# A fused adaLN, Mamba-2 and FFN kernel on one core: a new order of the last prologue steps and of the first unit's state updates

## The reference

```
mod = silu(c) @ wmod                                    # six rows of 512: sa ca ga sb cb gb
ga, gb = sign * max(|.|, 0.25)
h   = layernorm(x) * (1 + ca) + sa
proj = h @ in_proj_w.T                                  # gate 8192 | hBC 8192 + 1024 + 1024 | dt 128
hBC = silu(causal_conv4(hBC) + conv_b)                  # -> hs (128 heads x 64), B, C (8 groups x 128)
dt  = clip(softplus(dt + dt_bias), 0, 100);  A = -exp(A_log)
Y   = chunked scan, chunks of 128 tokens:
      Y_diag = (C B^T * L) (dt hs);  states = B^T (decay * dt hs);  Y_off = exp(A_cum) C state
y   = (Y + D hs) * silu(gate), RMS-normalised in 8 groups of 1024 channels, * norm_w
x   = x + ga * (y @ out_proj_w.T)
x   = x + gb * ((layernorm(x)*(1+cb)+sb) @ sign(ffn_w).T + ffn_b)
```

## Time and profile before

| | |
|---|---|
| median of three runs | 1803.72 us |
| profiled execution, its own time | 1806.34 us |
| its span, first to last instruction | 1804.5 us |
| TensorE matmul busy | 1738.3 us, 96% of the span |
| TensorE weight load busy | 1361.5 us, 75% |
| VectorE / ScalarE / GpSimd busy | 1379.1 / 1078.1 / 977.6 us |
| granted TensorE clock, mean | 0.985 of full |

### The profile page before, as it was taken

The page is one execution under the profiler, slowest core; times in us unless marked ns, Lnnn a source line. Parts: engine busy times, 40 slices in busy tenths (PEclk is TensorE's granted clock), DMA queues, the critical chain, the costliest instruction groups (busy, mean ns, idle before and its releaser), DMA issues.

```text
span 1804.5 us, 31771 instructions
## 1 busy us (share of the span) xinstructions
PE 1738.3 (96%) x9818; PEld 1361.5 (75%) x9818; DVE 1379.1 (76%) x2266; ACT 1078.1 (60%) x1830; POOL 977.6 (54%) x732
## 2 busy tenths in 40 slices
PE   6789999999999999999999999999999999999988
PEld 4567778777777777777787777777777777877776
DVE  4767788777877788777887778777887778876776
ACT  6556665666556666565656665566665656465553
POOL 1436474555546565355646555455754556676651
PEclk9899999999999999999999999999999999999989
DMA  6312121121212122021211212121210212221111
GB/s 229 103 37 70 50 79 45 36 68 56 80 29 74 45 66 63 27 74 56 68 52 36 69 50 79 29 74 51 69 55 26 74 56 74 78 62 60 51 47 59
DMA packets 80936, 112.97 MB, mean 63 GB/s; under 512 B 28402, under 2 KB 32498, under 8 KB 79988
## 3 DMA queue, kind: packets, MB, share of 16 engines
q1 hardware_dynamic: 62898, 78.24, 14.7%
q10 hardware_dynamic: 17858, 32.52, 5.4%
HBM read 88.42 MB, written 22.29 MB: 61 GB/s over the span
## 4 chain that ended last, share of the span: by engine, by line
issue 46%; POOL 36%; PE 10%; ACT 3%; DVE 2%; DMA 1%; SPq 1%; POOLq 1%; ACTq 0%; DVEq 0%
POOL yt L1798 10%; POOL ssq L1793 7%; POOL prev L1775 6%; POOL wg_lo L1700 4%; POOL wo_lo L1700 3%; POOL yt L1801 3%; POOL wx_lo L1700 3%; PE bank L506 2%; PE bank L508 2%; PE bank L507 2%; PE bank L895 1%; PE bank L767 1%; PE bank L902 1%; DMA gate<-w_mod_dram 0%; DMA dtw_d<-xdt 0%
## 5 line engine op out<-in xcount | busy, mean ns | idle before, releaser
L1798 POOL TENSOR_TENSOR yt<-yt,ea 128x384 f32<-128x384 f32 (+1 forms) x128 | 189.7, 1482 | 378.9 <-DVE ea L1608 378.9
L1578 DVE TENSOR_TENSOR lm<-lm,cbm 128x512 f32<-128x512 f32 x256 | 189.4, 780 | 147.7 <-ACT lm L1179 146.9
L1375 DVE SCALAR_TENSOR_TENSOR xc<-bank,bpar,xc 128x511 f32<-128x511 f32 (+2 forms) x384 | 285.3, 743 | 6.8
L506 PE MATMUL bank<-h_hi,wg_hi 128*128 128x512 f32 x640 | 262.0, 409 | 20.3 <-ACT gate L1104 10.4
L508 PE MATMUL bank<-h_hi,wg_lo 128*128 128x512 f32 x640 | 251.1, 392 | 0.0
L507 PE MATMUL bank<-h_lo,wg_hi 128*128 128x512 f32 x640 | 250.4, 391 | 0.0
L1775 POOL TENSOR_TENSOR prev<-prev,dec 128x512 f32<-128x512 f32 x96 | 130.5, 1360 | 154.7 <-DVE prev L1521 92.2
L506 PE MATMUL bank<-h_hi,wx_hi 128*128 128x512 f32 x512 | 211.2, 413 | 2.2 <-DVE bt L1375 2.2
L506 PE MATMUL bank<-wo_hi,g_hi 128*128 128x512 f32 x496 | 206.5, 416 | 0.0
L508 PE MATMUL bank<-h_hi,wx_lo 128*128 128x512 f32 x512 | 201.0, 393 | 0.0
L507 PE MATMUL bank<-h_lo,wx_hi 128*128 128x512 f32 x512 | 200.1, 391 | 0.0
(11 more groups left out here) (222 smaller groups left out, 3943.4 us busy)
## 6 DMA issues: line engine op xcount, KB each, us to landing
raw_w<-w_in_dram SPq DMA_DIRECT2D x145, 256.0 KB, 2.7
raw_w<-w_out_dram SPq DMA_DIRECT2D x64, 256.0 KB, 2.6
part_d<-part ACTq DMA_DIRECT2D x64, 256.0 KB, 2.1
part<-part_d ACTq DMA_DIRECT2D x60, 256.0 KB, 2.7
rt<-rows_d SPq DMA_DIRECT2D x256, 6.0 KB
acc<-x_dram SPq DMA_DIRECT2D x8, 256.0 KB, 6.9
acc<-w_mod_dram SPq DMA_DIRECT2D x2, 1024.0 KB, 6.1
lh<-neg_d SPq DMA_DIRECT2D x128, 6.0 KB
```

The source lines that it names most:

```text
L506: nc.tensor.matmul(out_ap, whi(k), hhi(k), start=(k == 0), stop=False)
L1375: stt(dst[:, at], ps[:, 0:HALF - 3 + k], w(k), dst[:, at], ALU.mult, ALU.add)\
L1578: tt(lm[:, h % 4, :], lm[:, h % 4, :], cbm[:, toks(hf)], ALU.mult).then_inc(v_m, 1)
L1798: tt(yt[:, j % 2, cols], yt[:, j % 2, cols], ea[:, j % 2, cols], ALU.add).then_inc(p_t3, 1)
```

## The change

Nothing is added or removed; the same instructions stand in another order.

- SyncE: weight fill 8 is issued ahead of the store of `dtw_d` and of the wait for it, fills 9 and 10 behind the last store of the decay rows and ahead of the wait for all these stores and of the 13 loads of `unit_params`.
- TensorE: projections 6 and 7 (x tiles 2 and 3) stand ahead of modulation row 5. In unit 0 the fourth gate projection and `gate_rows` stand ahead of state 0.
- ScalarE: the copy of row 5 stands behind the taps of x tiles 2 and 3; the weight splits 9 and 10 and the silu calls around them change places.
- VectorE: in unit 0 the low part of `xw` stands ahead of the state addition of the round before.
- GpSimd: weight tiles 9 and 10 are lowered ahead of the product for `gate_rows`.

```diff
--- before.py
+++ after.py
@@ -404,6 +404,7 @@
             store_rows(0, 1)
             sp.wait_ge(a_row, 7)
             store_neg(1)
+            pro_fill(8)
             sp.wait_ge(v_dtt, 4)
             sp.dma_start(dtw_d.rearrange("b t f w n -> t b (f w n)"),
                          flat(xdt, 0, 4).rearrange("t (b n) -> t b n", b=NBLK)).then_inc(d_scrt, 16)
@@ -411,18 +412,17 @@
             store_rows(0, 2)
             sp.wait_ge(d_scrt, 16)
             unit_steps(0, 0)
-            pro_fill(8)
             sp.wait_ge(p_split, 4)
             store_neg(2)
             sp.wait_ge(a_row, 8)
             store_rows(1, 1)
             sp.wait_ge(p_split, 5)
             store_rows(1, 2)
+            for n in range(9, FILLS0):
+                pro_fill(n)
             sp.wait_ge(a_const, 5)
             sp.wait_ge(d_scr, 16 * 20)
             unit_params(0, 0)
-            for n in range(9, FILLS0):
-                pro_fill(n)
 
             def x_tile(t):
                 if t >= 2:
@@ -613,10 +613,10 @@
             mod_row(4, 6)
             pro_item(5)
             to_tokens(1)
+            pro_item(6)
+            pro_item(7)
             te.wait_ge(a_mrow, 5)
             mod_row(5, 6)
-            pro_item(6)
-            pro_item(7)
             te.wait_ge(v_dtt, 4)
             for v in range(2, 6):
                 mod_columns(v, 4)
@@ -777,7 +777,8 @@
                 for z in range(NZ):
                     transposes(z)
                     if z == 2:
-                        gate_proj(g, c, 3)
+                        if not first:
+                            gate_proj(g, c, 3)
                         states(1)
                         continue
                     if z == 3:
@@ -796,9 +797,10 @@
                             if c in (0, 3):
                                 sum_squares(g - 1 if c == 0 else g, 1 if c == 0 else 0)
                     if z == 1:
+                        if first:
+                            gate_proj(g, c, 3)
+                            gate_rows()
                         states(0)
-                        if first:
-                            gate_rows()
 
                 items = early(proj_items(c, last))
                 order = [it for step in items for it in step]
@@ -1064,10 +1066,10 @@
             keep_row(4)
             pro_split(7)
             pro_tap(5)
-            keep_row(5)
             pro_split(8)
             pro_tap(6)
             pro_tap(7)
+            keep_row(5)
             def part_at(g, c):
 
                 return (g - 1, 1, 1) if c == 0 else (g, (c - 1) // 2, (c - 1) % 2)
@@ -1107,11 +1109,11 @@
             silu_x(0, 0)
             silu_x(0, 1)
             silu_c(0)
+            pro_split(9)
+            silu_gate(0, 0, 0)
             silu_x(0, 2)
-            silu_gate(0, 0, 0)
-            pro_split(9)
+            pro_split(10)
             silu_x(0, 3)
-            pro_split(10)
 
             def unit(g, c, last, first):
                 u, nb, hf = UPG * g + c, 2 * g + c // 2, c % 2
@@ -1555,11 +1557,13 @@
                         tt(by_head(xw[:, z % 2, :]), src, heads(dtw[:, hf], 1, z), ALU.mult).then_inc(v_xw, 1)
                     if z == 3 and not first:
                         accumulate(u, g1, b1, h1, 2, end)
-                    if z >= 1:
+                    if z >= 1 and not first:
                         new_state(z - 1)
                     if not last and z < NZ - hf:
                         ve.wait_ge(a_xh, sb0 + z + 1)
                         tt(xw_lo[:, z % 2, :], xw[:, z % 2, :], xw_hi[:, z % 2, :].bitcast(F), ALU.subtract).then_inc(x_lo, 1)
+                    if z >= 1 and first:
+                        new_state(z - 1)
                     if not first:
                         if z == 0:
                             group_sums(u, g1, b1, h1)
@@ -1743,11 +1747,10 @@
             tt(neg_parts[2], row_parts[1], fx, ALU.subtract).then_inc(p_split, 1)
             po.wait_ge(a_row, 8)
             tt(exp_parts[2], fy, exp_parts[1], ALU.subtract).then_inc(p_split, 1)
-            pro_lower(7, 9)
+            pro_lower(7, FILLS0)
             po.wait_ge(v_gval, 1)
             tt(flat(ea, 0, 2).rearrange("p (i n) -> p i n", n=128), ident[:, :].unsqueeze(1).broadcast_to((128, 2 * NK, 128)),
                small[:, 16:16 + 2 * NK].unsqueeze(2).broadcast_to((128, 2 * NK, 128)), ALU.mult).then_inc(p_diag, 1)
-            pro_lower(9, FILLS0)
             po.wait_ge(t_mrow, 6)
             nc.gpsimd.memset(flat(acc, 0, NT), 0.0).then_inc(p_zero, 1)
```

## The result

| | before | changed |
|---|---|---|
| median (6 runs each) | 1805.51 us | 1796.22 us |
| range | 1803.08 to 1807.29 | 1794.12 to 1798.02 |
| profiled execution, own time / span | 1806.34 / 1804.5 us | 1795.91 / 1794.1 us |
| mean granted clock | 0.985 | 0.989 |

The ratio is 0.9947, interval 0.9937 to 0.9957: 9.3 us off, 7.8 to 11.4. Forecast were 6.0 us off; the direction and the range held, the size was too small by a third. The forecast time, 1797.7 us, lies nearer to the measured 1796.22 than that only because the median of the kernel before is 1.8 us higher over six runs than over the three that the forecast started from.

The account below looks back on a forecast made before the run. TensorE, almost unbroken from 150 us, was taken as the bound, so only earlier time counted. Terms 3.3 + 2.44 + 0.7 - 0.5 = 5.9, say 6.0 us, gave 1803.72 - 6.0 = 1797.7 us; range 1794.0 to 1802.5.

Parts of the forecast that it names:

- The bound: From 150 us TensorE works almost without a break, so a shift of that stretch's entry shifts the end equally.
- Part 1: Prologue: two x projections ahead of modulation row 5 use most of TensorE's 4.48 us pause; gain 3.3 us.
- Part 2: Prologue: earlier fills 9 and 10 remove TensorE's whole wait ahead of the third gate projection; gain 2.44 us.
- the fills aren't there: Rival: fills 9 and 10 land past 89 us, the third gate projection's wait stays; 1800.1 us, chance 0.07.
- Part 3: Unit 0: the reordered chain puts the last state T + 14.0 behind the transposes, against 14.86; 0.7 us taken.
- The price against it: Unit 0: gaps ahead of states 2 and 3 make the clock fall earlier; a loss of 0.5 us, from 0 to 4.
- slower, by the states: Rival: clock falls at about 98 us in unit 0, low until about 125; 1807.7 us with Part 1 cold, chance 0.08.
- it goes deeper: Rival: the clock stays up through the columns and the states; up to 9 us, 1794.7 us, chance 0.08.
- The sum: Start of unit 1's x projections: 3.3 + 2.44 + 0.7 - 0.5 = 5.9, say 6.0 us, and the same at the end.
- The exchange on VectorE: Unit 0, low part before state addition: by VectorE/GpSimd exclusion worth nearly its cost; without it, about 1 us loss.

Follow-up runs that it names:

- `spread_columns`: Changed kernel with column products dealt out between gate projection k-steps, fills 9 and 10 ahead of the last neg_d stores: 1793.75 us.
- `old_unit0`: Changed kernel with unit 0 as before (fourth gate projection between states 0 and 1, state additions ahead of low parts): 1798.97 us.
- `warm_gaps`: Changed kernel with 6 unused matmuls ahead of state 2 and 6 ahead of state 3 of unit 0: 1794.70 us.
- `before_warm_gaps`: Kernel before with 4 unused matmuls ahead of state 2 and 6 ahead of state 3 of unit 0: 1804.60 us.
- `no_fill8`: Changed kernel with weight fill 8 back in its old place behind the load of step sizes: 1800.37 us.
- `both`: Changed kernel with `spread_columns`' edit, unit 1's first x projection ahead of unit 0's state 3, and 6 unused matmuls ahead of state 2: 1790.92 us.
- `old_row_order`: Changed kernel with modulation row 5 ahead of x projections 2 and 3, and its copy ahead of tile 8's split, as before: 1799.86 us.

## Why the prediction was right or wrong

- **The bound.** Right: the shift at 124 us (8.95) is there at 1547 us (8.70), and TensorE is as busy in the steady stretch (198.08 of 200 us). 0.25 us were lost on the way.
- **Part 1, 3.3 us.** Right in size: 76.92 - 73.19 - 0.26 = 3.5 us, and 3.3 when undone. The size has some luck in it. It was worked out from a return of the clock 3.5 to 4.4 us behind the start of dense work, and the clock does not go by that (last section); where it came back at 70.7 or 70.9 instead of 68.3, in `spread_columns` and `old_unit0`, row 5 started at 73.39 and 73.48 instead of 72.19, and 1.2 us of the gain were not there. Wrong was the sentence that the early fill 8 costs and brings nothing, "even as late as before": I looked at TensorE's gate projection, which was in time, and not at what the split holds up on ScalarE now that the row's copy stands behind it. Without that fill 4.16 us of wait appear.
- **Part 2, 2.44 us.** The wait went as forecast and the fills landed as forecast (83 to 85; their splits began at 82.90 and 84.43). But its price was read off as the wait's length in the kernel before. That holds only while nothing ahead of it moves. With part 1 done, the late fills would have waited away part 1 as well; with late fills the third gate projection starts only 0.5 us earlier than before, and the ratio is 0.9999. Parts 1 and 2 are worth some 6 us together and part 1 close to nothing alone. The rival "the fills aren't there", at 1800.1 us, counted part 1 as won; that kernel took 1804.87.
- **Part 3, 0.7 us.** A mis-sized term: 1.5 us, with the cost of the new low stretch in it. State 0 came 5.3 us behind the transposes and not 5.6, and a round took 3.19 us and not 3.35; the low parts took 0.69 us each and GpSimd's three decays 1.06 (1.56, 1.44 and 1.06 before).
- **The price against it, -0.5 us.** The step that failed. I had the clock fall earlier, which it did, and priced the new low stretch; that price was near (0.8 us by `warm_gaps`, and part 3's 1.5 has it in it already). But I set nothing against it for the old low stretch that goes away. That one lay over x projections, of which 2.5 us ran cold; the new one lies over short products that wait for others anyway. From the first x projection to the second off-diagonal product it is 6.01 us instead of 7.17: +1.2 where the sum has -0.5, a miss of 1.7 us. `old_unit0` (7.29) shows it again, and `before_warm_gaps` (5.99) that it is the clock's. The prediction knew of this cost, put it at 3.3 us in its rival "slower, by the states", and left it out of its own sum. What that rival feared, a low clock from 98 to 125, did not come: no low stretch of the 14 kernels outlasted 10.2 us.
- **The rival "it goes deeper".** Its 9 us are close to the 9.3, but by luck: the clock did not stay up through the columns and the states (low from 75.2 to 82.0 and from 102.5 to 109.3).
- **The sum.** At the second off-diagonal product, with the 0.26 us taken off: row and columns 3.5 - 0.4 (the columns took 5.1 us and not 4.7; the clock fell in their midst in both kernels, so why is open), from there to the B/C products 0.3, from those to the third gate projection 2.7, the chain of states 1.5, the clock behind it 1.2: 8.7 (the parts rounded), of which 8.4 are left in the last group, against 6.0. The rest of the 9.3 of the runs lies within their interval. The prediction read the falls of the clock before as 79.5 and 113.4 us; its windows give 79.1 and 113.2, but no term of the sum rests on these.
- **The exchange on VectorE.** Its mechanism, exclusion, is seen again in both kernels with the old order in the last rounds; the claim that the old order in rounds 2 and 3 costs nearly what it saves is right for state 3 (0.4 us) and the x projections (0.0).

## What to carry to other kernels

A wait is worth its length only if nothing ahead of it gets faster. Of two waits in a row the second swallows what the first gave, if what ends it comes no earlier; so removals are to be priced together and undone one by one. When an instruction is moved behind a load's consumer on its engine, that load can join the path. And a low clock costs by what lies in it: here 1.2 us for 2.5 us over dense matmuls, 0.8 for 6.8 us over a chain of short products that wait anyway. A low stretch that goes away is to be priced like one that comes. A stretch of pauses is best kept away from the start of dense work, or filled with some of that work.

## What the runs showed of the hardware

The column products of one column each did not keep the clock up, though TensorE counts as busy in them: in the twelve kernels where they stood in a row it fell 2.0 to 3.2 us after the first of them, or 5.2 where a wait parted them (`no_fill8`); dealt out between matmuls of 512 columns, in `spread_columns` and `both`, they left it high.

The clock's return is the second point. I had taken the clock's return for a delay behind the start of dense work (3.5 and 4.4 us in the prediction). The windows of all 14 kernels (the two compared and the twelve of the experiments) between 55 and 135 us say otherwise: of 41 low stretches 31 lasted 6.8 us, 7 lasted 3.4 and 3 lasted 10.2. Here the x projections began at 65.02 after a fall at 61.5 and had the clock back at 68.3; in `spread_columns` they began at 65.18 after a fall at 63.9 and had it back at 70.7, 6.8 us behind the fall in both. The two kernels with 10.2 us in the prologue, before and `old_row_order`, are those whose clock fell ahead of the pause of 4.5 us. What sets the moment of the fall stays open: with the instructions up to there unchanged it fell at 62.0 in the kernel before and at 66.5 in `before_warm_gaps`, and such shifts come on top of every comparison of two single traces here.
